# A post-norm transformer layer: keys and values projected two slots later, the store one slot later, and the high part of x1 first

## The reference

```python
qkv = x @ Wqkv + bqkv                  # 16 query heads of 16, 4 groups of keys and values
scores = einsum('bqhd,bkhd->bhqk', q, k) / 16
out = einsum('bhqk,bkhd->bqhd', softmax(scores), v) @ Wout + bout
x = layernorm(x + out)                 # x1
h = silu(gate) * up                    # gate, up = x @ ternary(w_gate_up).T, width 1024 each
x = layernorm(x + rms_norm(h) @ ternary(w_proj).T)
```

## Time and profile before

| what | value |
|---|---|
| median of 3 runs | 613.4 us (611.0 to 614.56) |
| the profiled execution's own time | 612.37 us |
| its span, first to last instruction | 610.5 us |
| PE busy | 557.7 us, 91% |
| DVE busy | 434.5 us, 71% |
| ACT busy | 370.4 us, 61% |
| POOL busy | 345.9 us, 57% |
| mean granted TensorE clock | 0.968 |
| DMA, queue of SP | 37.8% of 16 engines' span |

### The profile page before, as it was taken

One profiled execution on the slowest core, in us unless ns is written; L12 is line 12 of the kernel. 1 busy time (PEld: TensorE's weight loads), 2 busy tenths in 40 slices (PEclk: granted clock), 3 DMA queues, 4 the chain that ended last, 5 costly groups with the idle time before them and its releaser, 6 DMA issues.

```text
span 610.5 us, 14163 instructions
## 1 busy us (share of the span) xinstructions
PE 557.7 (91%) x4368; PEld 471.0 (77%) x4368; DVE 434.5 (71%) x1018; ACT 370.4 (61%) x738; POOL 345.9 (57%) x452
## 2 busy tenths in 40 slices
PE   5688999999999999999999999999999999999782
PEld 5677787778888888878787888888888877777672
DVE  6865866677778777777868777877777677855751
ACT  4444845666666666667575666766666666566441
POOL 4565761244736455555547374636555555566975
PEclk9687999999999999999999999999999999999986
DMA  6955265353353517160725344353517160101001
GB/s 215 152 134 70 77 93 111 57 102 66 78 106 79 105 47 139 45 129 16 156 28 130 52 99 84 77 104 73 109 45 137 39 127 3 37 2 37 19 0 35
DMA packets 53933, 49.08 MB, mean 80 GB/s; under 512 B 6145, under 2 KB 53889, under 8 KB 53889
## 3 DMA queue, kind: packets, MB, share of 16 engines
q1 hardware_dynamic: 51152, 47.60, 37.8%
q10 hardware_dynamic: 2736, 0.92, 0.7%
HBM read 33.29 MB, written 14.68 MB: 79 GB/s over the span
## 4 chain that ended last, share of the span: by engine, by line
PE 71%; DVE 15%; issue 5%; DMA 3%; POOL 2%; ACT 1%; ACTq 1%; SPq 1%; POOLq 0%; DVEq 0%
PE ffn_ps L460 17%; PE short_ps L460 11%; PE pv_ps L557 10%; PE short_ps L507 9%; PE exp_ps L516 7%; PE down_ps L542 7%; PE short_ps L565 5%; DVE gated L831 2%; DVE st L907 2%; PE ffn_ps L581 2%; DVE r L904 2%; DVE x1T_lo L778 2%; DVE row_max L789 2%; DVE h_f L838 1%; DMA wgu_raw<-in_L_ffn_w_gate_up_dram 1%
## 5 line engine op out<-in xcount | busy, mean ns | idle before, releaser
L789 DVE TENSOR_REDUCE row_max<-short_ps 128x2 f32<-128x512 f32 x256 | 174.0, 682 | 68.6 <-PE short_ps L507 68.4
L942 POOL TENSOR_TENSOR h_lo<-h_f,h_hi 128x256 fp32r<-128x256 f32 x128 | 94.8, 741 | 191.1 <-ACT h_hi L685 180.7
L703 ACT ACTIVATE probs<-exp_ps 128x1024 f32<-128x1024 f32 x128 | 131.1, 1024 | 35.5 <-PE exp_ps L516 33.4
L460 PE MATMUL ffn_ps<-x1T_hi,wguT 128*128 128x256 f32 x480 | 125.1, 293 | 16.2 <-DVE h_f L838 9.0
L507 PE MATMUL short_ps<-k_st,q_st 65*128 65x256 f32 x512 | 117.6, 312 | 9.2 <-DVE row_max L789 5.5
L460 PE MATMUL ffn_ps<-x1T_lo,wguT 128*128 128x256 f32 x480 | 119.5, 282 | 0.0
L694 ACT ACTIVATE tanh<-ffn_ps 128x256 f32<-128x256 f32 x120 | 45.9, 383 | 119.7 <-PE ffn_ps L460 103.0
L460 PEld LDWEIGHTS ffn_ps<-x1T_hi,wguT 128*128 128x128 f32 x480 | 90.9, 189 | 23.2 <-DVE h_f L838 11.0
L507 PEld LDWEIGHTS short_ps<-k_st,q_st 65*128 65x128 f32 x512 | 83.2, 194 | 19.2 <-DVE row_max L789 6.9
L460 PEld LDWEIGHTS ffn_ps<-x1T_lo,wguT 128*128 128x128 f32 x480 | 90.9, 189 | 0.0
L947 POOL TENSOR_TENSOR sq_sum<-sq_sum,h_sq 128x256 f32<-128x256 f32 x112 | 83.4, 744 | 0.0
(11 more groups left out here) (100 smaller groups left out, 907.7 us busy)
## 6 DMA issues: line engine op xcount, KB each, us to landing
q_st<-q_dram SPq DMA_DIRECT2D x128, 128.0 KB, 4.0
q_dram<-q_p SPq DMA_DIRECT2D x16, 512.0 KB, 3.0
xn<-in_L_attn_x_dram SPq DMA_DIRECT2D x16, 256.0 KB, 4.4
k_st<-k_dram SPq DMA_DIRECT2D x64, 64.0 KB, 2.6
res<-in_L_attn_x_dram SPq DMA_DIRECT2D x16, 256.0 KB, 3.1
out_dram<-y_out SPq DMA_DIRECT2D x16, 256.0 KB, 2.2
wgu_raw<-in_L_ffn_w_gate_up_dram SPq DMA_DIRECT2D x8, 256.0 KB, 7.2
k_dram<-k_p SPq DMA_DIRECT2D x16, 128.0 KB, 3.1
```

The costliest lines, as they stand in the source:

```text
L460: last = pe.matmul(dst, a, b, start=start and i == 0, stop=stop and i == len(pairs) - 1)
L703: act.activation(probs[:, st.s % 4], exp_ps[:], ACT.Exp).then_inc(exp_done, 1)
L789: dve.tensor_reduce(row_max[:, st.par, head * TT:(head + 1) * TT], short(n, f"max{i}")[:].rearrange("p (t k) -> p t k", t=TT), AX.X, ALU.m ...
L942: pool.tensor_tensor(h_p[1][:, st.s % 4, :], h_f[:, st.s % 2, :], h_p[0][:, st.s % 4, :].bitcast(F32), ALU.subtract).then_inc(h_lo, 1)
```

## The change

Keys and values are projected, copied, split and saved in slot 4 instead of slot 2; saving queries and saving keys are now two steps with semaphores of their own, and the key stacks wait for the keys' save. The last layer norm's reciprocal root goes from slot 2 to slot 3, its application and the store from slot 4 to slot 5. `gate_up` does its four matmuls on the high part first and waits for the low part only before the other four. The bank table is written anew for the moved projection: banks 1 and 2 change roles in slots 0, 1, 5, 6 and 7, and the keys' product has bank 2 in slot 4.

```diff
-PROJ_K = 2
-SAVE_QK = 2
+PROJ_K = 4
+SAVE_Q = 2
+SAVE_K = 4
...
-LN2_APPLY = 44
-STORE = 44
+LN2_APPLY = 45
+STORE = 45
...
-K_COPY = 2
-K_LOW = 2
+K_COPY = 4
+K_LOW = 4
...
-RSTD2 = 42
+RSTD2 = 43
...
-              2: {"max0": 0, "q": 2, "max1": 0, "k": 1, "att": 2},
+              2: {"max0": 0, "q": 1, "max1": 0, "att": 2},
               3: {"max0": 0, "max1": 1, "o": 2},
-              4: {"max0": 1, "max1": 0},
+              4: {"max0": 1, "max1": 0, "k": 2},
...
             def stack_keys(st):
+                sp_wait(k_saved[st.par], st.count2(16, 16))
                 for c in range(4):
...
-                if st := n.once(SAVE_QK):
+                if st := n.once(SAVE_Q):
                     sp_wait(q_lo, st.count(1, 1))
-                    sp_wait(k_lo, st.count(1, 1))
                     sp_wait(q_stacked[0][st.par], st.count2(64, 0))
                     sp_wait(q_stacked[1][st.par], st.count2(64, 0))
+                    sp.dma_start(q_dram[st.par].rearrange("a (m p) t -> p a m t", p=P), q_p[:].bitcast(F32)
+                                 ).then_inc(q_saved[st.par], 16)
+                if st := n.once(SAVE_K):
+                    sp_wait(k_lo, st.count(1, 1))
                     sp_wait(k_stacked[st.par], st.count2(64, 0))
...
+                    if st.it is None and st.b == 0:
+                        stack_keys(st)
...
             def gate_up(n, st):
-                wait(pe, x1T_lo, st.count(1, 1))
+
+                wait(pe, x1T_hi, st.count(1, 1))
...
-                for half in range(2):
-                    c = half * F + st.s * P
-                    last = products(gate_up_bank(n, st, half),
-                                    [wguT[:, k, c:c + P] for k in range(DT) for _ in range(2)],
-                                    [x1T[a][:, st.par, k, :] for k in range(DT) for a in range(2)])
+                for a in range(2):
+                    if a:
+                        wait(pe, x1T_lo, st.count(1, 1))
+                    for half in range(2):
+                        c = half * F + st.s * P
+                        first = a == 0 and (half == 0 or alternate(n, st))
+                        for k in range(DT):
+                            last = pe.matmul(gate_up_bank(n, st, half), wguT[:, k, c:c + P], x1T[a][:, st.par, k, :],
+                                             start=first and k == 0, stop=a == 1 and k == DT - 1,
+                                             skip_group_check=True)
```

More of the change, by code:

```diff
@@ L93 @@
               if name not in SHORT_OFFSET or SHORT_OFFSET[name] % SLOTS == m]
-BANK_TABLE = {0: {"max0": 2, "pv1": 0, "max1": 1, "sq": 2},
-              1: {"max0": 1, "x": 0, "max1": 2, "shift1": 1},
-              2: {"max0": 0, "q": 2, "max1": 0, "k": 1, "att": 2},
+BANK_TABLE = {0: {"max0": 1, "pv1": 0, "max1": 2, "sq": 1},
+              1: {"max0": 2, "x": 0, "max1": 1, "shift1": 2},
+              2: {"max0": 0, "q": 1, "max1": 0, "att": 2},
               3: {"max0": 0, "max1": 1, "o": 2},
-              4: {"max0": 1, "max1": 0},
-              5: {"max0": 2, "shift0": 0, "max1": 1, "x1": 2},
-              6: {"max0": 0, "pv0": 1, "max1": 0},
-              7: {"max0": 2, "v": 0, "max1": 1}}
+              4: {"max0": 1, "max1": 0, "k": 2},
+              5: {"max0": 1, "shift0": 0, "max1": 2, "x1": 1},
+              6: {"max0": 0, "pv0": 2, "max1": 0},
+              7: {"max0": 1, "v": 0, "max1": 2}}
 BANK = {(m, name): BANK_TABLE[m][name] for m, name in SHORT_USES}
@@ L313, in postln_layer @@
         v_made, v_copied = sem("v_made"), sem("v_copied")
-        qk_saved = [sem(f"qk_saved{i}") for i in range(2)]
+        q_saved = [sem(f"q_saved{i}") for i in range(2)]
+        k_saved = [sem(f"k_saved{i}") for i in range(2)]
         q_stacked = [[sem(f"q_stacked{h}_{i}") for i in range(2)] for h in range(2)]
@@ L407, in slot @@
                                  ).then_inc(x_loaded[st.par], 16)
-                if st := n.once(SAVE_QK):
+                if st := n.once(SAVE_Q):
                     sp_wait(q_lo, st.count(1, 1))
-                    sp_wait(k_lo, st.count(1, 1))
                     sp_wait(q_stacked[0][st.par], st.count2(64, 0))
                     sp_wait(q_stacked[1][st.par], st.count2(64, 0))
+                    sp.dma_start(q_dram[st.par].rearrange("a (m p) t -> p a m t", p=P), q_p[:].bitcast(F32)
+                                 ).then_inc(q_saved[st.par], 16)
+                if st := n.once(SAVE_K):
+                    sp_wait(k_lo, st.count(1, 1))
                     sp_wait(k_stacked[st.par], st.count2(64, 0))
-                    sp.dma_start(q_dram[st.par].rearrange("a (m p) t -> p a m t", p=P), q_p[:].bitcast(F32)
-                                 ).then_inc(qk_saved[st.par], 16)
                     sp.dma_start(k_dram[st.par].rearrange("a p t -> p a t"), k_p[:].bitcast(F32)
-                                 ).then_inc(qk_saved[st.par], 16)
+                                 ).then_inc(k_saved[st.par], 16)
+                    if st.it is None and st.b == 0:
+                        stack_keys(st)
                 if st := n.once(LOAD_RES):
@@ L422, in slot @@
                 if st := n.once(STACK_QK):
-                    sp_wait(qk_saved[st.par], st.count2(32, 32))
+                    sp_wait(q_saved[st.par], st.count2(16, 16))
                     sp_wait(exp_scored, st.count(8, -12))
-                    if st.it is None and st.b == 0:
-                        stack_keys(st)
                     stack_queries(st, 0)
@@ L715, in slot @@
                     if st.it is not None or st.b > 0:
-                        wait(act, qk_saved[1 - st.par], Step(st.b - 1, 0, st.it).count2(32, 32))
+                        wait(act, q_saved[1 - st.par], Step(st.b - 1, 0, st.it).count2(16, 16))
                     wait(act, q_read, st.count(1, 1))
@@ L743, in slot @@
                     wait(act, v_made, st.count(1, 0))
+                    if st.it is not None or st.b > 0:
+                        wait(act, k_saved[1 - st.par], Step(st.b - 1, 0, st.it).count2(16, 16))
                     act.activation(kv_f[:], short(n, "k")[:, 0:S], ACT.Identity, bias=bkv[:, 0:1])
```

## The result

The changed kernel takes 624.46 us (median of 4 runs, 623.68 to 626.49). The kernel before took 612.2 us beside it (4 runs, 610.69 to 614.56). The ratio is 1.0215, 95% interval 1.0185 to 1.0245: slower by 2.1%. The forecast was 621 us, with a range of 606 to 631. The profiled execution took 625.08 us with a span of 623.3, against 612.37 and 610.5 before.

What follows compares the result with a forecast made beforehand. PE was taken as the bound, busy 31.80 of a batch's 32.77 us. The profiled 612.4 us, +3.0 start-up, -1.0 early gates and projections, +9.0 ten circles, -2.1 end gave 621.3; forecast 621 us, range 606 to 631.

Steps and rivals of the forecast that it cites:

- The circle: From one transpose of x to the next, through y_out, store and stacks: 33.7 us against 32.77, +0.9 in ten batches, +9.0.
- the clock: Rival: PE's clock falls at each wait for x, up to 3.4 us each, 34 in ten batches, 655 us; chance 0.05.
- The landing: Load of x on SP's queue lands a median of 4.5 us after its issue (3.7 to 6.7), so PE waits.
- the rival of x in time: x lands before slot 1's transposes want it at 441.0, each of ten batches gains 0.65: 605.8 us; chance 0.18.
- The high part first: Slot 7's gate-and-up product starts its four matmuls on x1T_hi before x1T_lo is there: gain 0.47 us per batch.
- Keys and values: Projection on PE leaves slot 2 (0.87 us, 0.4 won) for slot 4, whose next product starts 0.2 us earlier than before.
- The copies: K_COPY on ACT in slot 4, K_LOW on DVE before slot 5's row maximum: costed at nothing, else up to 0.2 us per batch.
- The start: Batch 0's keys come later behind pieces of weights, first maximum scores start 4 us later: +3, bounds +1 and +5.5.
- The end: High-first product of slots 127, 135, 143 and 151, each 0.47 us, and the last projection: -2.1 us.
- The bounds: The forecast's own case was put between 614 and 630 us.

Runs made afterwards that it cites:

- the bank experiment: The changed kernel with the store in slot 4 and banks 0 and 1 exchanged for slot 3's two groups of maximum scores: 600.87 us, ratio 0.9819.
- the first experiment: The changed kernel with the layer norm's last step and the store back in slot 4, all else kept: 606.63 us, ratio 0.9935 to the kernel before.
- The first two experiments: The changed kernel with the layer norm's last step and store back in slot 4 (606.63 us), and with only the store's issue moved to slot 8 (606.42 us).

## Why the prediction was right

**The circle (+9.0 predicted, +12.4 measured).** Every link came as worked out: y_out behind h_lo and sq_sum, ending 23.2 us after the transposes (predicted 23.3); 5.69 us from the store's issue to that of x in the batch shown (4.8 to 6.4 over the ten; predicted 5.55); x landing 3.7 to 5.3 us after its issue, with a median of 4.7 over line 409's fourteen loads and 4.6 over these ten (predicted 4.5). Seven circles took 33.1 to 33.9 us, 33.48 on average, against 33.7 predicted. That is +0.70 each. The three others took 35.11, 35.30 and 35.49. In each of them the granted clock was 0.50 for 3.41 us, which at half speed is 1.7 us, and y_out ended 24.7 to 24.9 us after the transposes instead of 23.1 to 23.3. So the term is 10 x 0.70 = 7.0 of waiting and 3 x 1.82 = 5.5 of clock.

**What the sum left out** is the clock, to which the prediction gave one chance in twenty as something that happens at each wait or not at all. It happened at three of ten, and cost about half of the 3.4 us each that were its upper bound. These 5.5 us are more than the 3.8 us by which the profiled execution (625.1) lies above the sum (621.3): without them, by an estimate, it would have taken 619.6, and the waiting alone was 2.0 less than the +9.0 of the sum. That the total came so near is in part luck, two errors of opposite sign. The clock is not what makes the kernel slower: the kernel before with the output's slot alone had waits of the same kind and no such fall, and took 1.9% longer.

**The landing.** Over all its loads x took a median of 4.6 us and the residual, of the same 256 KB, 3.2; eight stacks are issued just ahead of x and one store just ahead of the residual. The Trainium skill (DMA: Bandwidth & Descriptors, section Queues, rings and completion order) says that on each DMA engine the descriptors of a queue are consumed in the order of its ring; the two medians agree with that. Taking the trace's median was right, and with it the rival of x in time fell.

**The high part first.** 0.54 us per batch alone, 0.47 predicted.

**Keys and values.** 0.4 of the 0.87 was to be won in slot 2 and 3 together. In the changed kernel slot 2 became 0.90 shorter and slot 3 0.46 to 0.69 longer (5.74 to 5.97 against 5.28), so 0.2 to 0.4 was won; the bank experiment shows that it is the bank. Slot 4 was to be 0.2 longer; it is 3.23 instead of 3.02 to 3.12. The two edits together were costed at 0.65 us per batch if x is in time, with a sum of 605.8; the first experiment is that case, with 0.77 (batches of 32.00 on average) and 605.1 for its profiled execution (606.6 for the median of its runs). The copies cost nothing that shows.

**The start.** +3.0, as taken; that it fits to a tenth is luck. The first gate-and-up product came at 103.5 to 105.1 us in the three traces with the start of before, and at 108.1 to 109.9 in the five with the changed start; the means lie 4.8 apart, still inside the bounds of +1 and +5.5. The first maximum scores started at 29.88 (predicted 30.4). Inside the sum two errors partly cancel: the save went at 22.32 instead of 23.4, because K_LOW took 0.41 us and stood ahead of the next piece, and the first key stack followed it by 3.74 instead of 3.07, because the save landed (26.05) behind the last of the query stacks that now go ahead of it (25.86). That is the bound of the step, "if the query stacks, sent ahead now, hold the save up", in a smaller size. The wait for the shift's DMA in slot 15 shrank from 1.19 to 0.75.

**The end (-2.1 predicted, -1.4 measured).** The four last high-first products were costed at 0.47 each. What slot 3's wait takes from the last batches was left out: with the bank mended the stretch from slot 127 on takes 110.8 us against 111.5 in the first experiment.

**The bounds.** The low end of 614 is not the sum of the low bounds: 612.4 + 1.0 - 1.0 + 1.0 - 2.1 is 611.3. The high bounds do give 630. The time lies inside either way.

## What to carry to other kernels

An engine that issues transfers in order makes every wait at its head a wait of all that stands behind it: before moving a late producer's store, follow that queue to the next load and compare its slack (here 1.4 to 2.4 us) with the delay (2.7 to 2.9). When one engine carries all the work, a gain on it is kept only if the circle through the other queues is shorter than the new batch; the share of busy time doesn't show this (90% in the losing kernel), the chain and the slack of each load do. Where a moved step leaves a gap, look at which buffer the next step takes: it may inherit the wait that the step had covered.

## What the runs showed of the hardware

Short waits in dense work went with a fall of the clock sometimes, not always. The order of time on PE at four of the changed kernel's waits for x:

```profile
282.04 0.30 PE L575 MATMUL short_ps<-ident,xn 128*128 128x128 f32 x1 [1.55 <-DMA xn<-in_L_attn_x_dram]
...
351.01 0.45 PE L575 MATMUL short_ps<-ident,xn 128*128 128x128 f32 x1 [1.55 <-DMA xn<-in_L_attn_x_dram]
386.31 0.44 PE L575 MATMUL short_ps<-ident,xn 128*128 128x128 f32 x2 [1.62 <-DMA xn<-in_L_attn_x_dram]
453.24 0.47 PE L575 MATMUL short_ps<-ident,xn 128*128 128x128 f32 x1 [1.15 <-DMA xn<-in_L_attn_x_dram]
```

Around 282.04, 351.01 and 453.24 the granted clock was 0.50 (1.2 GHz) for 3.41 us, from 282.56, 350.82 and 453.22 on. Around 386.31 it stayed at 1.00, though that wait was longer than the other three; so it did after the waits of 1.39 and 1.64 us in two other circles, and after all ten waits for x of 0.29 to 1.54 us in the kernel before with the output's slot alone. The first two experiments, which have no such waits, kept 1.00 from 63 to 572 us. The length of the wait alone doesn't tell at which the clock falls; what else decides stays open. What a fall costs is read from two circles, the first with one, the second without:

```profile
282.04:317.14 35.10, 33.43 (x256) 27.51 (x256) 24.79 (x60) 21.29 (x43) 18.18 (x25) 0.95 0.41 81
386.31:419.93 33.62, 31.93 (x256) 26.86 (x257) 24.80 (x60) 21.36 (x43) 18.16 (x25) 1.00 0.40 83
```

PE is busy 1.50 us longer with the same 256 matmuls, and the circle is 1.48 us longer. The Trainium skill (TensorE: Matmul & The Clock Gate, section HAM oscillation) describes a clock that falls at the wait of every tile, in a kernel whose waits for a DMA are about 3 to 5 us. So it is not just this case, as the prediction put it: the ten waits here were 0.98 to 1.64 us, and the clock fell at three of them.
